# Row scatters of the last group, one pair behind each of four result scatters, with a cleared tile ahead of late scatters

## What is computed

```python
x = x + tanh(g_xattn[0]) * xattn(ctx_2048, layernorm(x), mask, mask)   # 8 heads of 16, output projection of [target, update]
x = x + tanh(g_ffn[0])   * ffn(layernorm(x))                           # 9 experts, 2 chosen for each token

# ffn, on the 2048 rows x_flat
scores = sigmoid(x_flat @ gate.T + bias)
top_scores, selected = top_k(scores, 2);  top_scores /= sum(top_scores) + 1e-20
for e in range(9):
    h = silu(x_flat @ w1[e].T) * (x_flat @ w3[e].T)                    # 128 -> 352
    out += weight_of(token, e) * (h @ w2[e].T)                         # 352 -> 128
```

## Time and profile before

| what | value |
|---|---|
| median of 3 runs (lowest, highest) | 218.2 us (217.81, 218.67) |
| span of the profiled execution | 234.1 us |
| the profiled execution's own time | not given beside its span |
| busy: PE, PEld, DVE, ACT, POOL | 205.4, 166.9, 149.6, 142.7, 128.8 us |
| mean granted clock of PE | 0.968 |
| chain that ended last: PE, DVE, unknown, ACT, DMA, issue, POOL | 56, 14, 7, 6, 6, 5, 4% |

### The profile page before, as it was taken

How to read it: one execution, slowest core, us unless ns; L and a number is a source line. 1 busy time by engine, 2 the same in 40 slices (tenths; PEclk the granted TensorE clock), 3 DMA queues, 4 the chain that set the end, 5 groups by cost and what they waited for, 6 DMA issues and landing times.

```text
span 234.1 us, 5788 instructions
## 1 busy us (share of the span) xinstructions
PE 205.4 (88%) x1606; PEld 166.9 (71%) x1606; DVE 149.6 (64%) x523; ACT 142.7 (61%) x399; POOL 128.8 (55%) x230
## 2 busy tenths in 40 slices
PE   8999986999999999898883946299999999999981
PEld 3577653666666676565573945299999999999881
DVE  0469997788898698897865822344443444456774
ACT  2286869988778876786471620266667666666210
POOL 4237745132325876786783578556675756557320
PEclk9999999999999999999998897589999999999998
DMA  5999999999910100011372221121222221261194
GB/s 164 368 377 242 407 381 409 408 370 318 342 55 13 36 23 26 23 36 38 86 214 62 61 76 49 41 53 55 61 69 68 52 65 47 49 218 53 37 348 163
DMA packets 23602, 34.91 MB, mean 149 GB/s; under 512 B 2562, under 2 KB 15879, under 8 KB 23443
## 3 DMA queue, kind: packets, MB, share of 16 engines
q1 hardware_dynamic: 20610, 29.27, 37.9%
q0 software_dynamic: 2240, 4.23, 5.5%
q10 hardware_dynamic: 720, 1.02, 1.5%
HBM read 15.85 MB, written 19.06 MB: 149 GB/s over the span
## 4 chain that ended last, share of the span: by engine, by line
PE 56%; DVE 14%; another core or an unknown queue 7%; ACT 6%; DMA 6%; issue 5%; POOL 4%; SPq 1%; POOLq 0%; DVEq 0%; ACTq 0%
PE pt_ps L1363 10%; PE score_ps L1321 5%; PE pt_ps L1372 4%; PE score_ps L1323 4%; PE score_ps L1322 4%; PE score_ps L1176 4%; DMA kheads<-y_rows 3%; PE pt_ps L1116 3%; PE ps_a L1226 3%; PE pt_ps L1214 3%; PE score_ps L1126 2%; PE ps_b L1283 2%; DVE less L827 2%; ACT probs L401 2%
## 5 line engine op out<-in xcount | busy, mean ns | idle before, releaser
L616 POOL DMA_INDIRECT y_rows<-vals,ids x38 | 37.8, 995 | 17.2 <-ACT vals L473 9.6
L1363 PE MATMUL pt_ps<-w,probsT 128*128 x234 | 34.4, 285 | 14.6 <-ACT probsT L480 6.7
L1363 PEld LDWEIGHTS pt_ps<-w,probsT 128*128 128x128 f32 x234 | 32.1, 198 | 15.9 <-issue 15.8
L593 POOL DMA_INDIRECT x_rows<-stage,slot x32 | 32.7, 1022 | 10.4 <-issue 7.7
L401 ACT ACTIVATE probs<-score_ps,less 128x128 f32<-128x128 f32 x128 | 37.9, 419 | 0.4 <-DVE less L827 0.4
L1043 DVE TENSOR_TENSOR xg_low<-ps_a,xg_high 128x128 fp32r<-128x128 f32 x40 | 11.7, 291 | 37.1 <-issue 23.6
L473 ACT ACTIVATE vals<-pt_ps,xg 128x128 f32<-128x128 f32 x38 | 14.0, 368 | 34.4 <-PE pt_ps L1363 24.7
L1321 PE MATMUL score_ps<-w_high,xg_low 128*128 x80 | 30.3, 379 | 0.0
L1051 DVE TENSOR_TENSOR probs<-probs,score_ps 128x352 f32<-128x352 f32 x40 | 20.8, 521 | 11.2 <-PE score_ps L1323 5.3
L1323 PE MATMUL score_ps<-w_high,xg_high 128*128 x80 | 26.6, 332 | 0.0
L1322 PE MATMUL score_ps<-w_low,xg_high 128*128 x80 | 26.5, 332 | 0.0
(11 more groups left out here) (179 smaller groups left out, 445.6 us busy)
## 6 DMA issues: line engine op xcount, KB each, us to landing
x_rows<-pads SPq DMA_DIRECT2D x1, 9945.0 KB, 37.3
w_low<-in_w13T SPq DMA_DIRECT2D x3, 1056.0 KB, 11.0
xg<-x_rows SPq DMA_DIRECT2D x40, 65.0 KB
ctx_r<-in_ctxT SPq DMA_DIRECT2D x4, 512.0 KB, 7.7
y_rows<-pads SPq DMA_DIRECT2D x1, 2048.0 KB, 16.6
w<-in_w2T SPq DMA_DIRECT2D x1, 1728.0 KB, 11.2
kheads<-y_rows SPq DMA_DIRECT2D x3, 512.0 KB, 5.0
mask_b<-in_mask SPq DMA_DIRECT2D x4, 256.0 KB, 8.0
```

The lines of the kernel that those rows point to most:

```text
L593: pool.indirect_dma_start(x_rows[:, :], bass.IndirectOffsetOnAxis(ap=slot[:, par, c, p:p + 1], axis=0), stage[:, par, c, p, :], None, boun ...
L616: pool.indirect_dma_start(y_rows[:, :], bass.IndirectOffsetOnAxis(ap=ids[:, s:s + 1], axis=0), yt[:, s, :], None, bounds_check=last_row, o ...
L1363: last = nc.tensor.matmul(into[:, 0:D], hidT[:, q3, c, :], w2[:, bass.ds(e3, 1), c, :].rearrange("p o d -> p (o d)"), start=(c == 0), stop ...
```

## The change

It does three things, all on POOL. The eight row scatters of the last group no longer follow the result of tile 1 in one go; a pair of them follows the result of each of tiles 1 to 4. Every row scatter of groups 2 and 3 (16 indirect DMAs) has a clear of the whole spare tile ahead of it (`space(SPACE)`, 384 columns of bf16), which the scatter waits for. And the short clear ahead of a result scatter is made for all 38 results, not for the first 24.

```diff
+SPACE = 3 * D
...
-        minus_half, minus_one, spare = sb("minus_half", [P, UN]), sb("minus_one", [P, UN]), sb("spare", [P, 3 * D], BF16)
+        minus_half, minus_one, spare = sb("minus_half", [P, UN]), sb("minus_one", [P, UN]), sb("spare", [P, SPACE], BF16)
...
                 for c in copies:
+                    if g >= NG - 2:
+                        space(SPACE)
                     pool.indirect_dma_start(x_rows[:, :], bass.IndirectOffsetOnAxis(ap=slot[:, par, c, p:p + 1], axis=0), stage[:, par, c, p, :], None,
                                             bounds_check=last_slot, oob_is_err=False).then_inc(st_rows[p] if g < NG - 1 else st_last[p], 16)
...
-                if k < 3 * TR:
-                    short_space()
+                short_space()
                 pool.wait_ge(y_done, k + 1)
...
             for k in range(NT - SUMMED):
                 tile(k, k % TR)
-                if k == 1:
-                    for p in range(UN):
-                        scatter(NG - 1, p)
+                if 1 <= k <= UN:
+                    scatter(NG - 1, k - 1)
```

## The result

The changed kernel takes 226.91 us, the median of 4 runs (226.33 to 227.92), against 218.0 (217.69 to 218.67) for the kernel before beside it: a ratio of 1.0398, 95% interval 1.0355 to 1.0442, which is 7.7 to 9.6 us more. The forecast was 224.2, range 213 to 228.

A forecast was written before the change was run, and what follows sets the result against it. Without holds, PE sets the pace through the tile loop, with the last result scatter and reload behind it. 0.2 + 4.2 + 1.8 - 0.2 = +6.0 us on 215.9 + 2.3 gives 224.2 us, range 213 to 228.

The forecast's parts named there:

- The holds: Three PE idle times beside dense indirect DMAs on POOL: 18.2 us of the profiled execution, almost absent from timed runs.
- A: Rival: holds sit in the timed runs too and the clears end them; faster, 207 or 213 us; chance 0.27.
- B: Rival: runs have holds, and POOL's longer unbroken work lengthens them; 225 to 229 us; chance 0.12.
- The gate: SP loads tile 16 only after the last group's eighth row scatter lands; 9.5 us later, PE idle +4.2 us (1 to 7).
- Rival C: Tiles reach number 16 later than reckoned, or clears take 0.21 us, so its load is in time; 218 us; chance 0.13.
- the 4.49 us from the scatter to PE: Time from a last row scatter over landing and tile load to PE's first use, read at the first tile.
- The clock: PE's granted clock falls to 0.50 behind the wait at tile 16: +1.8 us (0 to 3.7).
- The third group: Its 8 clears delay the second norm's last reciprocal root: +0.2 us (0.1 to 0.5); tile 8 still in time.
- The tail: Clears ahead of results 24 to 37 let the last scatter start sooner after its result: -0.2 us (-0.5 to +0.3).
- The price of a clear: A 384-column clear takes 0.43 us on POOL, 0.33 more per row scatter (0.1 to 0.5); its whole price is POOL's order.

The follow-up runs named there:

- experiment 1: The kernel before, unedited, profiled a second time: 217.88 us, span 216.1 us.
- experiment 4: The kernel before with the short clear ahead of results 24 to 37 too, nothing else: 217.9 us, ratio 0.9985.
- experiments 6 to 8: Changed kernel with 22 unread products on PE ahead of tile 16, 224.78 us; changed kernel unedited, 228.09 us; kernel before with third group's clears alone, 218.5 us.
- experiment 2: Changed kernel with the last group's row scatters in one go behind tile 1's result and no clears for results 24 to 37: 220.39 us, ratio 1.0124.
- experiment 5: Changed kernel with row clears of 768 columns instead of 384, 231.07 us, and of 128 columns, 222.48 us.
- experiment 7: The changed kernel, unedited, profiled a second time: 228.09 us.

## Why the prediction was right, and which terms were off

**The holds** are not in the timed runs. The frame without them was put at a span of 215.9; the second profile has 216.1, and 47 runs of the kernel before in these sets lie between 216.56 and 219.81. (The 18.2 us of the prediction are 4.05 + 0.7 + 13.43: of the 1.97 it counts 0.7 as held.) What lies around the span is 1.8 us, not 2.3. Rivals A and B, which both needed holds in the runs, fall. I had given A 0.27: the 15.9 us by which one profile exceeded the median spoke against it from the start.

**The gate** is the mechanism, as forecast: an eighth scatter that comes too late for tile 16. Its position was nearly right. From the kernel before to the changed one it moved by 9.9 us against the mark (30.6 in experiment 1, 40.5 after), where the sum had 9.5; the clear's 0.43 us fits, and the gap of 0.71 instead of 0.63 is the 0.28 from a clear's end to a row scatter where I had used the 0.17 of a result scatter. Rival C, a gate that isn't late, falls.

**The step that was mis-sized is the 4.49 us from the scatter to PE**. From the eighth scatter it took 155.00 - 148.94 = 6.06, and 5.4 to 6.2 in the other kernels. Two parts differ from the first tile's. The landing took 3.17 instead of 2.30 us. And between landing and load stand 0.94 us (148.94 + 3.17 to 153.05) where the first tile has 0.24 (109.27 + 2.30 to its load at 111.81): in the code SP reads the first tiles' places in the table ahead of the gate, but tile 16's (`value_load`) behind it. In SP's part of the chain the `value_load` (L319) takes 152.33 to 152.86, 0.53 of the 0.94. Together the two parts are 1.57 of the 6.06. No run moved the `value_load`, and why the landing takes longer (2.60 to 3.17 in these kernels) stays open. The nearest row was of the same pair of transfers, yet not of the same code around them. With 6.06 for 4.49, the forecast wait of 4.2 would have been 5.8; it was 5.5. That this fits so well is in part luck: counted from the mark, the eighth scatter came 0.6 us later than summed (40.5 against 39.9) and PE wanted tile 16 0.9 us later (41.1 against 40.2), and the two nearly cancel. The room in the kernel before was off in the same way, 4.0 us instead of 5.1.

**The clock** cost 2.65 us, with another 0.26 of starting up; forecast 1.8, bounds 0 to 3.7.

**The third group**: forecast +0.2, measured 1.0003 (0.9974 to 1.0032), so 0 with about 0.6 us either side. DVE's use of the last root, 9.65 us behind the mark in experiment 4, came 9.65 to 9.86 behind it in the profiles with 384 columns (experiments 6 to 8): at most 0.2 later. In all of these the clock falls to 0.50 about there; where it stays at 1.00 the use comes at 9.45 without clears (experiment 1) and at 9.46 with them (experiment 2).

**The tail**: forecast -0.2, in the trace -0.09; the last scatter starts 0.67 us after its result in the changed kernel too, where the prediction looked for 0.3 to 0.5. Its mechanism, that the scatter now holds the wait for the result, was there but idle, since POOL's own work ends later than the result. The ids copy ends with DVE's row choice and the clear comes behind both. So the question on which I had weighed the Trainium skill ("SBUF — State Buffer", section "Who interferes with whom") did not arise at the tail: no row there has a clear beside the row choice. Earlier in the changed kernel a clear of 384 columns (133.21 to 133.65) covers a short DVE instruction with two SBUF inputs (L935 at 133.44), and both keep their usual 0.44 and 0.16 us, which agrees with that section of the Trainium skill. The Trainium skill says there too that of two instructions that contend for the shared port pair one is blocked until the other ends; the ids copy that starts within the row choice and takes 0.51 to 0.56 instead of 0.20 us agrees.

**The price of a clear**, which the prediction put at POOL's order alone, is more than that for 768 columns: about 3.7 us of DVE's time on the path (experiment 5). With 384 columns two such steps of DVE take 0.58 and 0.53 instead of 0.15 and 0.16 us, beside row scatters, and the tiles around them keep their period of 2.06 us.

Sum of what the profile shows: 5.5 + 2.9 + 0 - 0.1 = 8.3 us, against 7.7 to 9.6 measured. The forecast of +6.0 was too low by 1.3 at the gate and 1.1 at the clock.

## What to carry to other kernels

A part moved or added on an engine off the critical path is paid from the room of the gate behind it. Work out that room first, with the instructions that stand between that gate and the engine it feeds (the landing, the waiting engine's own reads, the load), each read at that place and not at a similar one. Two edits that each look free can use the same room; test them together, and let a change of one size (here the clear's length) show whether the gate is already late. Where a profiled execution lies far from the timed runs, profile again before arguing from it.

## What was not expected of the hardware

- **Holds in one execution.** In the first profile DVE and ACT waited up to 6.04 us, beside dense indirect DMAs, for signals that the profile calls remote; in the second profile of the same kernel, with the same gaps of 0.30 us, there was no such wait, nor in any other of this study. What sets it off wasn't tried.
- **The loss by the clock doesn't grow with the wait.** Idle times of 0.68, 1.46 and, behind the 22 products, 0.74 us left the clock at 1.00 behind them; 3.23 cost 1.87 us, 5.36 cost 2.91, but 6.90 only 1.80 (loss behind the wait, start-up included; one profile each, and 2.97 after 5.23 in experiment 7). In the stretches behind them the mean granted clock was 0.72 after 3.23 and 0.69 after 6.90, 6 us each.
- **The clock also falls without the change.** From 116 to 118 us it was 0.50 in four of the thirteen profiles, 0.65 and 0.71 in the two of the changed kernel, and 1.00 in the other seven; experiments 1 (1.00) and 4 (0.50) have the same code ahead of it. Tile 15 comes 38.0 us after the mark in the one and 39.1 in the other.
- **DVE steps that end with a clear or a row scatter of POOL.** With 768 columns four TENSOR_SCALARs of DVE took 1.07 to 1.23 us instead of 0.16 to 0.34, each ending with a clear (experiment 5). In the changed kernel L933 took 0.58 instead of 0.15 us and ended with a row scatter (133.22). Other steps beside clears and scatters kept their length; what decides it wasn't tried.
